# A graph network on one core: edge features of the gathered groups computed once, during the maximum pass

## What is computed

```python
# x: (12500, 64), edge_attr: (212500, 32), five layers l
for l in range(5):
    h = leaky(x @ W1[l] + b1[l]) @ W2[l] + b2[l]
    e = leaky(edge_attr @ We1[l] + be1[l]) @ We2[l] + be2[l]      # edge features
    agg = segment_sum(h[src] * e * dot_scale[l], dst)
    x = layernorm(x + agg * res_w[l]) * ln_g[l] + ln_b[l]
```

## Time and profile before

| | |
|---|---|
| median of the runs | 14682.35 us |
| span of the profiled execution, first to last instruction | 14665.5 us |
| maximum pass, of it | about 586 to 2682 us |
| attention pass | about 2700 to 4000 us |
| one hybrid pass, the work between two layers included | about 1291 us, five times |
| busy over the span: TensorE, VectorE, ScalarE, GpSimd | 77%, 67%, 45%, 62% |

### The profile page before, as it was taken

How to read it: one execution, slowest core, us unless ns; L and a number is a source line. 1 busy time by engine, 2 the same in 40 slices (tenths; PEclk the granted TensorE clock), 3 DMA queues, 4 the chain that set the end, 5 groups by cost and what they waited for, 6 DMA issues and landing times. The chain is left out here.

```text
span 14665.5 us, 407711 instructions
## 1 busy us (share of the span) xinstructions
PE 11315.1 (77%) x130415; PEld 10362.9 (71%) x130572; DVE 9799.3 (67%) x18666; ACT 6661.0 (45%) x12964; POOL 9154.8 (62%) x9382
## 2 busy tenths in 40 slices
PE   0366666589566787878699979989997998899585
PEld 0244444488555787878599979978997998899585
DVE  8777777567799323232477777787777778777624
ACT  0000000122266555555466656656665665666454
POOL 0377777677497675757366656656665666666474
PEclk9877776555567999999899999999999999999798
DMA  3122222222167565556444434434443443444463
GB/s 116 33 56 56 56 57 56 57 76 81 52 246 255 184 204 164 197 165 202 118 140 136 138 100 137 138 95 141 138 138 100 137 138 102 135 137 137 121 201 117
DMA packets 1278373, 1854.38 MB, mean 126 GB/s; under 512 B 539494, under 2 KB 806630, under 8 KB 1276774
## 3 DMA queue, kind: packets, MB, share of 16 engines
q1 hardware_dynamic: 995393, 1495.07, 32.6%
q0 software_dynamic: 276480, 306.10, 9.3%
q10 hardware_dynamic: 5040, 35.13, 0.6%
HBM read 1526.62 MB, written 308.76 MB: 125 GB/s over the span
## 5 line engine op out<-in xcount | busy, mean ns | idle before, releaser
L1183 POOL DMA_INDIRECT rows_buf<-feature_table,idx_buf x3680 | 3780.4, 1027 | 1977.3 <-issue 1199.8
L880 POOL DMA_INDIRECT rows_buf<-feature_parts,idx_buf x2176 | 2054.3, 944 | 960.8 <-issue 357.5
L919 ACT ACTIVATE sums_space<-banks 128x384 bf16<-128x384 f32 x3920 | 1658.9, 449 | 1263.5 <-PE banks L936 1236.9
L936 PE MATMUL banks<-table_parts,tmp 128*128 128x192 bf16 x13720 | 1786.1, 248 | 365.9 <-DMA tmp<-one_hots 365.4
L734 POOL DMA_INDIRECT rows_buf<-attention_table,idx_buf x1664 | 1571.1, 944 | 554.2 <-issue 554.2
L1280 PE MATMUL banks<-attr_buf,params 128*128 128x256 f32 x5900 | 1663.1, 405 | 274.8 <-DMA attr_buf<-cell_attr 164.4
L949 PE MATMUL banks<-sums_space,tmp 128*128 128x192 bf16 x13720 | 1782.3, 247 | 0.0
L1235 ACT ACTIVATE sums_space<-onehot 128x448 bf16<-128x448 f32 (+1 forms) x1475 | 875.7, 594 | 1971.7 <-DVE onehot L1374 728.2
L1291 PEld LDWEIGHTS banks<-params,hidden 128*128 128x128 f32 x11800 | 1562.9, 193 | 95.0 <-DVE hidden L1359 17.8
L1291 PE MATMUL banks<-params,hidden 128*128 128x128 f32 (+1 forms) x11800 | 1533.7, 274 | 8.3 <-DVE hidden L1359 7.1
L1303 PE MATMUL banks<-table_parts,tmp 128*128 128x64 bf16 x42630 | 1435.8, 194 | 115.6 <-issue 115.6
(11 more groups left out here) (385 smaller groups left out, 20260.7 us busy)
## 6 DMA issues: line engine op xcount, KB each, us to landing
tmp<-one_hots SPq DMA_DIRECT2D x1995, 448.0 KB
attr_buf<-cell_attr SPq DMA_DIRECT2D x1015, 128.0 KB
one_hots<-tmp SPq DMA_DIRECT2D x245, 448.0 KB
attr_buf<-attr SPq DMA_DIRECT2D x573, 128.0 KB
rows_buf<-feature_table,idx_buf POOLq DMA_INDIRECT x3680
gathered_rows<-rows_buf SPq DMA_DIRECT2D x208, 272.0 KB, 2.1
rows_buf<-gathered_rows SPq DMA_DIRECT2D x208, 272.0 KB
rows_buf<-feature_parts,idx_buf POOLq DMA_INDIRECT x2176
```

What stands on the lines that cost most here:

```text
L880: pool.indirect_dma_start(out=far_rows[:, u, t, :], out_offset=None, in_=table3, in_offset=bass.IndirectOffsetOnAxis(ap=idx_buf[:, u, t:t ...
L919: act.activation(cell_rows[:, q, 0:width], bank[q][:, 0:width], ACT.Copy).then_inc(s_cells_sb, 1)
L936: ins = pe.matmul(bank[q][:, j % 2 * 3 * D:(j % 2 + 1) * 3 * D], src_cells[:, k, j, side * P:(side + 1) * P], table_parts[:, 2 * (k * CELL ...
L1183: pool.indirect_dma_start(out=edge_rows[:, u, t, :], out_offset=None, in_=table, in_offset=bass.IndirectOffsetOnAxis(ap=idx_buf[:, u, t:t ...
```

## The change

The edge features of the 92 gathered groups are computed for all five layers during the maximum pass, written to memory as f32 (256 KB for a group and layer), and loaded by the hybrid passes in place of the attributes (128 KB). The diff, cut to its core; first the hybrid pass:

```diff
+                def far_load(g, slot):
+                    sp.dma_start(far_edge[slot], of_group(features, first + (g + base))).then_inc(s_attr[2 + slot], 16)
...
                 def turn(w, w_ahead, tail=False):
+                    if not (tail and w.g + 2 >= HF):
+                        sp.wait_ge(s_mult, w.n + 1)
+                        sp.sem_inc(s_turn, 1)
+                        far_load(w.g + 2, w.slot)
...
-                    if w_ahead:
-                        put_bias(w_ahead, early)
+                    if w_ahead and w_ahead.near:
+                        put_bias(w_ahead)
                         copy_hidden(w_ahead)
...
-                    if w_ahead:
-                        hidden_layer(w_ahead, early and w_ahead.n < 2)
-                    if w_later:
+                    if w_ahead and w_ahead.near:
+                        hidden_layer(w_ahead)
+                    if w_later and w_later.near:
                         edge_features(w_later)
...
-                    e = edge_bank(w).rearrange("p (t d) -> p t d", d=D)[:, 0:w.tiles, :]
+                    e = (edge_bank(w) if w.near else far_edge[w.slot]).rearrange("p (t d) -> p t d", d=D)[:, 0:w.tiles, :]
...
-                    if w_ahead:
+                    if w_ahead and w_ahead.near:
                         leaky(w_ahead)
```

Then the maximum pass, whose first 46 turns (184 groups) carry ten feature computations each, m = 0 to 459. Each is a `hidden_layer` into bank 5, a ScalarE copy, a leaky step on VectorE, a bias by ScalarE and `edge_features` into bank 6 or 7, a ScalarE copy out, and a store of 256 KB. An even group has two of them and an odd group three:

```diff
 TensorE
+                    for k in range(4): (inside spread, after the pair of tiles k)
+                        if beside:
+                            beside(k)
...
+                    if m is not None:
+                        made_here = (((0, "edge"), (1, "hidden"), (1, "edge"), (2, "hidden")),
+                                     ((2, "edge"), (3, "hidden"), (3, "edge"), (4, "hidden"), (4, "edge"), (5, "hidden")))[u % 2]
 VectorE
+                    dve.tensor_tensor(
+                        not_hot[:, slot, :, :], max_numbers,
+                        max_key[:, bass.ds(g * G, G)].unsqueeze(1).broadcast_to([P, P, G]), ALU.not_equal).then_inc(s_hot, 1)
...
+                    if m is not None:
+                        n = (0, 2)[u % 2]
+                        leaky(m + n, side_of(u, n))
                     b = block_of_group(dve, g)
...
+                    for k in range(4):
+                        pair_maximum(g + 1, k)
+                        if m is not None and (u % 2, k) in ((0, 2), (1, 0), (1, 2)):
+                            n = {(0, 2): 1, (1, 0): 3, (1, 2): 4}[u % 2, k]
+                            leaky(m + n, side_of(u, n))
 ScalarE, even group (the odd one likewise, with 2, 3 and 4 taken)
+                        taken(0)
+                        begun(2)
+                        copied(1)
+                        next_transposed()
+                        taken(1)
+                        begun(3)
+                        copied(2)
 SyncE
+                    for n in ((0, 1), (2, 3, 4))[u % 2]:
+                        keep_features(f, n, m + n, side_of(u, n))
```

More of the change, by code:

```diff
@@ L87, in param_columns @@
     }
-Work = namedtuple("Work", "near n begins side own adds follows_near s k g u round tiles slot attr loads chunk")
+Work = namedtuple("Work", "near n begins side own adds follows_near c back s k g u round tiles slot loads chunk")
 class Steps:
@@ L1074, in build, with near_between, two_near_back @@
         ALL_ADDS = adds
+        NEAR_A_TURN = sum(1 for n in range(TURN) if is_near(n))
+        def near_between(a, b):
+            return sum(1 for n in range(a, b) if is_near(n))
+        def two_near_back(n):
+            left, at = 2, n
+            while left:
+                at -= 1
+                left -= is_near(at)
+            return n - at
         ADDS_A_TURN = own_of[TURN] - own_of[0]
@@ L1100, in work, with through, hybrid_pass @@
             return Work(near=False, s=None, k=None, g=i * per + f, u=f % U, round=i * (per // U) + (f // U + 1), tiles=G, slot=f % 2,
-                        attr=2 + f % 2, loads=i * (per // 2) + (f // 2 + 1), chunk=None, **common)
-        def hybrid_pass(block):
+                        loads=i * (per // 2) + (f // 2 + 1), chunk=None, **common)
+        def through(w, pos, ahead, tail=False):
+            m = pos + (TURN * TURNS if tail else 0)
+            return w.c + near_between(m, m + ahead + 1)
+        def hybrid_pass(block, features, base):
             far_bank, strip_bank = bank[1], bank[6]
@@ L1163, in turn @@
                         hot_chunk(w.s + 1, w.k)
-                    else:
+                        return
+                    if not (tail and w.g + U >= HF):
                         sp.wait_ge(s_rows[w.u], w.round * (16 * G))
@@ L1215, in _ @@
                         if is_far(pos):
[L1216 removed]
+                            group_behind(work(i, pos), pos)
                 for pos in range(TAIL):
@@ L1289, in edge_features @@
                             t, at = 4 * half + 2 * pair, (2 * pair + half) * P
-                            end = min(t + 2, CELLS if w.near and w.k >= 2 else G)
-                            ins = pe.matmul(edge_bank(w)[:, t * D:end * D], hidden[:, w.side, at:at + P], w2[:, 0:(end - t) * D],
+                            end = min(t + 2, CELLS if w.k >= 2 else G)
+                            ins = pe.matmul(edge_bank(w)[:, t * D:end * D], hidden[:, w.slot, at:at + P], w2[:, 0:(end - t) * D],
                                             start=False, stop=(half == 1 and pair == 1), skip_group_check=True)
@@ L1339, in _ @@
                 for pos in range(-4, 0):
-                    turn(None, work(0, pos + 2) if pos >= -2 else None, work(0, pos + 4), True)
+                    turn(None, work(0, pos + 2) if pos >= -2 else None, work(0, pos + 4))
                 with pe.Fori(0, TURNS) as i:
@@ L1586, in transpose_parts, with hidden_layer, edge_features, spread @@
                                  ident_bf[:, :]).then_inc(s_tr, 1)
-                def spread(g, slot, between):
+                def hidden_layer(m, n, slot, loads, early=False):
+                    if n == 0:
+                        pe.wait_ge(s_attr[slot], loads * 16)
+                    if not early:
+                        pe.wait_ge(s_act_hid, m)
+                    for pair in range(2):
+                        ins = pe.matmul(bank[5][:, pair * 2 * P:(pair + 1) * 2 * P], layer_of(n, "We1")[:, pair * P:(pair + 1) * P],
+                                        attr_buf[:, slot, :, :].rearrange("p a e -> p (a e)"), start=True, stop=True)
+                    ins.then_inc(s_hid, 1)
+                def edge_features(m, n, side):
+                    pe.wait_ge(s_leaky, m + 1)
+                    pe.wait_ge(s_biased, m + 1)
+                    for half in range(2):
+                        for pair in range(2):
+                            t, at = 4 * half + 2 * pair, (2 * pair + half) * P
+                            ins = pe.matmul(made_bank(side)[:, t * D:(t + 2) * D], hidden[:, side, at:at + P], layer_of(n, "We2"),
+                                            start=False, stop=(half == 1 and pair == 1), skip_group_check=True)
+                    ins.then_inc(s_edge, 1)
+                def spread(g, slot, between, beside=None):
                     pe.wait_ge(s_hot, g + 1)
```

307 lines of the change are left out of this document (237 added, 70 removed).

## The result

The kernel after takes 14913.76 us (median; 14912.76 to 14914.8), the kernel before 14678.2 us in the same comparison. The ratio is 1.0161 with a 95% interval of 1.0146 to 1.0175: 236 us slower. The forecast was 14925.

A forecast was written before the change was run, and what follows sets the result against it. It took the gather to bound the maximum pass and the VectorE, ScalarE, VectorE chain the hybrid passes. 14682 - 180 (hybrid passes) + 418 (maximum pass) + 5 (weights) = 14925 us; range of 8 in 10: 14600 to 15200.

The forecast's parts named there:

- The ring of the maximum pass: Maximum pass: pieces going TensorE, ScalarE, VectorE, TensorE in queue order become the new bound, 11.6 us a group at full clock.
- the walk: Maximum pass: steps summed over a pair of groups, 23.2 us; L0 to L4 are leaky steps, P0 to P3 maxima.
- The allowance of 1.3 us a pair: Maximum pass: added to the 23.2 us a pair for pieces running at half clock, giving 12.25 us a group.
- The term was +418: Maximum pass: 184 groups at 12.25 us instead of the gather's 9.98 add 418 us.
- The term was -180: Hybrid passes: shorter turns ahead of far units, 161 us, and loop turns, 19 us, save 180 together.
- 0.35: Hybrid passes: mean us saved for each of 92 far units in five passes, 161 us in all.
- 19 us at the loop turns: Hybrid passes: one hidden layer of 0.76 us less before the multiply after each of 25 loop turns.
- VectorE's wait for the middle part: Hybrid passes: sign that VectorE would wait about 0.7 us for ScalarE's middle part in turns ahead of a far unit.
- Gather as the bound: Maximum pass rival: gather stays the bound, 14507 to 14632 us; 0.27 together with a larger gain in the hybrid passes.
- The break-even of 10.9 us a group: Maximum pass: below 10.9 us a group the whole change gains.
- Half clock: Maximum pass rival: TensorE at half clock throughout, 15.9 us a group, +1089 us, 15596 us; chance 0.08, half clock or nearly.
- TensorE as the bound of the hybrid passes: Hybrid passes rival: up to 782 us less there, 14323 us in all; no separate chance, within the 0.27 for faster.

The follow-up runs named there:

- the new order: Kernel after with the maximum pass's pieces reordered on TensorE, VectorE and ScalarE, no work left out: 14611.92 us, ratio 0.9955 to the kernel before.

## Why the prediction was right

**The bound before.** The gather bounds the maximum pass: the masks alone made one gather in eight 0.23 us longer, and the time moved by the sum of it. The hybrid pass is bound by the chain of VectorE and ScalarE: relieving TensorE gave nothing, filling a gap of VectorE gave 17 us a pass.

**The ring of the maximum pass.** The steps of the walk, as measured in one pair:

| step | predicted | measured |
|---|---|---|
| L0 to P0 | 2.26 | 2.65 |
| P0 to L1 | 3.64 | 3.57 |
| L1 to P3 | 2.81 | 2.82 |
| P3 to L2 | 1.74 | 1.74 |
| L2 to L3 | 4.45 | 4.47 |
| L3 to L4 | 4.68 | 4.67 |
| L4 to L0 | 3.60 | 3.91 |
| pair | 23.2 | 23.8 |

The mean over all pairs of the pass is 23.9. The ring is right within 3%. The allowance of 1.3 us a pair for pieces at half clock was wrong: the granted clock was 1.00 from 1000 to 2000 us. The walk was 0.6 us short and the allowance 1.3 us too long, so that 11.94 us a group came instead of 12.25. The term was +418 and measured +363. The 5 us for the weights and the start of the pass measured 6.8. That the mechanism is order and not load, which the walk said and the busy sums could not, is shown by the new order: 302 us came back with every instruction still there. The clock of 1.00 came with TensorE 76% busy, less than the 94% at which the attention pass stays at 0.50. The Trainium skill's rule that the prediction weighed ("TensorE: Matmul & The Clock Gate", on what is actually happening: activity releases the throttled default) gives the right clock for this pass, and does not say by itself why the attention pass stays low.

**The hybrid passes.** The term was -180 with bounds of -120 and -300. It measured -157 alone and -132 within the kernel after. Three turns of a strip of ten stand two ahead of a far unit. From one multiply to the next, over four passes and without the loop turns, they fell in the kernel after from 3.63 to 3.15 us (predicted 3.21), from 4.15 to 3.73 and from 3.59 to 3.33. But the turn of near 0 rose from 4.25 to 4.59, since its high part now mostly waits for TensorE's addition (48 of 72 times; not once before). The net is 0.27 us for each far unit, and 0.30 in the passes alone: 0.35 was too much. The other part, 19 us at the loop turns, came with some 16 us when the passes were changed alone, and not in the kernel after: the three turns at a loop turn take 17.2 us in the kernel before, 16.6 in the passes alone and 17.4 in the kernel after. VectorE's wait for the middle part, 0.7 us in turns ahead of a far unit, is there as said.

**A term that was missing.** The prediction adds the two stages as if they did not touch each other. They do. First to last rest of high, five passes, by the traces:

| | hybrid passes of before | hybrid passes of the change |
|---|---|---|
| maximum pass of before | 6326.6 | 6166.3 |
| maximum pass of the change | 6375.4 | 6194.4 |

Within the larger program the change of the hybrid passes is worth 181 us, which is the forecast; but the larger program itself costs them 49 us (or 160 and 28, taken in the other order), a term that the prediction does not have. In the first four passes it is 13.6 us a pass for the old text and 6.5 for the new (1137.2 against 1130.7), of which 8 to 10 us are TensorE's stands at the loop turns; the old text's fifth pass gains 10. So two errors of size offset each other: the maximum pass was costed 55 us too high, and the hybrid passes were forecast to save 48 us more than they did. That 14925 came within 11 us of 14914 is in that part luck.

**At nothing.** The stores cost nothing, as costed (15090 without stores, 15105 with them and in another comparison; ratios 1.0277 and 1.0279). The load of the features was not tried alone; in the trace of the kernel after VectorE is never idle before the multiply of a far unit (L1417, 0.0 us over 88 of them). SyncE's waits "add nothing" held too, though they show as 135 us of gathers waiting for indices: with the ring cured, they are gone. The masks' price of nothing was wrong by 48 us in a pass bound by gathers. In the kernel after, where the ring is the bound, GpSimd is idle for a third of the time, so that a stretched gather should cost little there; that was not tried alone. In the new order the pass is still 63 us longer than before, and the stretched gathers are about 50 of them. By their count the leaky steps have as much part in that as the masks.

**The rivals.** Gather as the bound gave 14507 to 14632 us in the prediction, and the new order lands there with 14612. The break-even of 10.9 us a group fits as well: 11.94 lost, 10.26 won. Half clock and TensorE as the bound of the hybrid passes are both refuted by runs.

## What to carry to other kernels

When work is put beside a stage that another engine bounds, busy sums say only whether it could fit. Write down the ring of steps through the queues for one period and add it up. If it comes out over the present bound, look for a place where an engine waits for a piece while other pieces that it could do are queued behind, and swap those two: here a hidden product moved ahead of an edge product, and the copy and the leaky step with it, was worth 302 us, and turned a loss of 236 us into a gain of 68. When a step leaves a chain of two engines, look at what wait it had covered, and put an independent step of the same length there.

## What was not expected of the hardware

A VectorE operation with both inputs in on-chip memory lengthens a GpSimd gather that runs beside it (the bf16 comparison: 1.18 us mean against 0.946, up to 1.46; the f32 leaky step up to 1.47); the comparison with one input in a bank does not (0.943 us). The Trainium skill ("SBUF — State Buffer", who interferes with whom) states that a VectorE instruction with two SBUF inputs contends with GpSimd's reads, and these runs agree. It also infers that such an instruction leaves descriptor generation alone. The gathers are indirect DMAs, and they were held. A gather reads its indices from on-chip memory too, and whether that reading or its descriptors were held, the traces do not tell apart.

TensorE stands at the loop turns of an unchanged stage for 30.9 us a pass in place of 21.1 when another stage of the program is larger, while in the copy of the stage behind the loop over the layers it stands for 19.5 us in place of 28.0. What in the larger program does this was not tried alone and stays open.
